# The first three passes of a software-pipelined attention and expert kernel in another order: loads of the first tile's keys and values ahead of the next tile's stores, split weights made in the third pass

## The chip, the cores and the metric

The kernel runs on one core of one Trainium2 chip. The metric is the device time of one execution in microseconds (us); lower is better. A core has five engines, each with its own instruction queue: TensorE (PE, with its weight loads shown apart as PEld), VectorE (DVE), ScalarE (ACT), GpSimd (POOL) and SyncE (SP), which here issues nearly all DMAs. Engines meet only at semaphores.

## The reference, cut to what matters

`x` is 4 x 2048 x 256 in fp32. Two blocks follow each other, each with a residual:

```python
x = x + attn(_layernorm(x))     # below
x = x + ffn(_layernorm(x))      # 8 experts, the best 2 by a gate on the mean over the sequence

def attn(q_x):                  # 16 heads of 16
    xn = ln(q_x, ln1_w, ln1_b)
    q, k, v = (xn @ w + b for w, b in ((wq, bq), (wk, bk), (wv, bv)))
    fq, fk = elu(q) + 1, elu(k) + 1
    kv = einsum('bhnd,bhne->bnde', fk, v)        # over the heads of one position
    qkv = einsum('bhnd,bnde->bhne', fq, kv)
    qk = einsum('bhnd,bnd->bhn', fq, fk.sum(axis=1))
    a = (qkv / (qk[..., None] + 1e-6)) merged to (b, n, 256)
    x = q_x + a @ wo + bo
    h = gelu(ln(x, ln2_w, ln2_b) @ fc_w + fc_b)  # 256 -> 1024
    return x + h @ proj_w + proj_b
```

## The kernel before, in words

The 8192 positions are cut into 16 tiles of 512. The work on a tile is cut into named stages, and a pass (`iterations`, L59) is a list of stage names; `LAG` (L44) says how many passes behind the pass number the tile of a stage is, so one pass holds early stages of one tile, middle stages of the tile before, and so on. The order is written out by hand. `walk` (L153) goes through all passes and stages, and every engine's program is made by one such walk: an engine takes from each stage the part that is its own, in this one order. A wait is on a count that the walk keeps (`at(name)`): the number of increments of that semaphore by all stages that stand earlier in the order, whatever tile they belong to. So the place of a stage also decides what its waits cover.

The stages that matter here, by tile (t is the tile's number):

- `L:t` SP loads the input tile. `DS:t`, `D1:t`: DVE statistics and normalisation into `xhat` (L598), POOL the power -1/2 (L423).
- `X:t`: PE transposes `xhat` into the PSUM banks `sa` (L828), ACT copies them to `xhT` (L470).
- `DV:t`: PE makes the values in `sa` (L872), ACT copies them to `feat_v` (L480) after a wait on `v_out` (L477), that is on all value stores so far, since there is one `feat_v`; POOL adds the bias (L430); SP stores them to `scratch_v` in 8 DMAs (L327).
- `DQ:t`, `DK:t`: PE makes queries (banks `pw`) and keys (banks `sa`) (L881), ACT the two halves of elu (L488, L489), DVE joins them in `fqk` (L651), SP stores them to `scratch_q`, `scratch_k`, 2 DMAs each (L333).
- `K0:t`, `K1:t`: SP loads one half of the queries and keys back in another layout, 8 DMAs (L356), after waits on all stores `q_out` and `k_out` that stand earlier in the order (L351-352). `VL:t`: SP loads the values back into `vb`, 8 DMAs (L345), after `v_out` (L337).
- `B0`, `B8`: PE makes the scores of the first half (L892) in the four banks of `ps`, which are `sa` and `sb`; DVE masks them into `am` (L658). `B1`: the weighted sum of the first half into `sa` (L905), ACT to `ot` (L513). `B2`: scores and mask of the second half. `B3`: its weighted sum.
- `NS0`, `NS1`: SP stores a half of `ot` to `scratch_nd` (L363). `NL0`, `NL1`: SP loads it back as numerators and denominators `nd`, 3 DMAs (L369). `N0`: DVE divides the first half; `N`: the second half, then the split of `attnT` (L687, L690, L697, L698).
- `Y`, `YB`: the residual (DVE, POOL). `A2:t`: PE multiplies with `wo` (L986), DVE adds and takes statistics. `R`, `H`, `SA`: second norm, its transposes (L828), the sum on POOL.
- `M1` to `M4` (from the fourth pass on): the MLP of one tile (L936 up, L920 down) together with B1 to B4 of the next. `F1` to `F2`: experts.
- `WV`: once, the bias of the values. `WS`: once, the MLP bias with `ln2_b` folded in (PE, 32 small matmuls, L850, after which DVE adds them at L631), `ln2_w` folded into `fc_w` (L633), and `wo`, `fc_w` and `proj_w` split into two fp32r parts each (L641, L643). `A2` of tile 0 waits for the splits (`split_done`).

The first passes hold fewer stages than the later ones, since the pipeline fills. The lag of `K0`, `K1`, `VL`, `B0`, `B8` is 1 and that of `Y`, `A2`, `N` and the like 2, so pass 2 is the one in which tile 0 reaches `A2` and pass 3 is the first with the MLP. In pass 2, `B1` to `B3` and `NS0` to `NL1` are those of tile 0, `VL`, `K0`, `K1` those of tile 1, and `X`, `DV`, `DQ`, `DK` those of tile 2.

Of the kernel before, what the change touches and what calls it, by code (L numbers as in the profile page):

```python
# [8 lines left out]
H, HD = 16, 16  # L9
# [7 lines left out]
SUB = T // P  # L17
# [23 lines left out]

LAG = {"L": 0, "DS": 0, "D1": 0, "X": 0, "DV": 0, "DQ": 0, "DK": 0, "K0": 1, "K1": 1, "VL": 1, "B0": 1, "B8": 1,  # L44
       "Y": 2, "YB": 2, "NS0": 2, "NL0": 2, "NS1": 2, "NL1": 2, "N0": 2, "N": 2, "A2": 2, "R": 2, "SA": 2, "H": 2, "J7": 3, "JA": 3, "XS": 4, "J2": 4, "Z": 4, "E": 4,
       "XL": 7, "F1": 7, "F3": 7, "F4": 7, "FX": 7, "F2": 7}
TAIL = ["DV", "DQ", "DK", "A2", "F1", "R", "B0", "F3", "F4", "SA", "H", "B8", "FX", "F2"]
HEAD_TAIL = ["XL", "E", "X", "J7", "JA", "YB", "G", "N", *TAIL]
FULL_TAIL = ["XL", "X", "J7", "JA", "YB", "E", "N", *TAIL]
MERGED = ["L", "XS", "M1", "J2", "Y", "NS0", "M2", "NL0", "K0", "DS", "Z", "M3", "NS1", "D1", "M4", "NL1", "VL", "N0", "K1"]  # L50
EARLY = ["L", "M1", "Y", "NS0", "M2", "NL0", "K0", "DS", "M3", "NS1", "D1", "M4", "NL1", "VL", "N0", "K1", "X", "J7", "JA", "YB",
         "N", "DV", "DQ", "A2", "R", "DK", "SA", "B0", "B8", "H"]


def experts(t):
    return [f"F1:{t}", f"F3:{t}", f"F4:{t}", f"FX:{t}"]


def iterations():  # L59

    yield 0, ["WV", "DS:0", "L:1", "D1", "X", "DV", "DS:1", "DQ", "L:2", "D1:1", "DK"]
    yield 1, ["X", "K0", "WS", "VL", "DV", "DQ", "DS:2", "DK", "D1:2", "B0", "B8", "K1"]
    yield 2, ["K0", "Y", "B1", "NS0", "X", "DV", "B2", "NL0", "DQ", "B3", "NS1", "NL1", "VL", "N0", "K1",
              "DK", "YB", "N", "A2", "R", "SA", "B0", "B8", "H"]
    yield 3, EARLY
    for i in range(4, 7):
        yield i, [
            s for t in EARLY for s in {"L": ["L", "XS"], "Y": ["J2", "Y"], "M3": ["Z", "M3"], "YB": ["YB", "E"]}.get(t, [t])]
    for i in range(7, TILES):
        yield i, MERGED + (HEAD_TAIL if i % PER_BATCH == PER_BATCH - 1 else FULL_TAIL)  # L70
    yield 16, ["XS", "M1", "J2", "Y", "NS0", "M2", "NL0", "K0", "Z", "M3", "NS1", "M4", "NL1", "VL", "N0", "K1", "XL",
               "J7", "JA", "YB", "E", "N", "F1", "F3", "F4", "A2", "R", "SA", "B0", "B8", "H", "FX", "F2"]
    yield 17, ["XS", "M1", "J2", "Y", "NS0", "M2", "NL0", "Z", "M3", "NS1", "M4", "NL1", "N0", "XL",
               "J7", "JA", "YB", "E", "N", "F1", "F3", "F4", "A2", "R", "SA", "H", "FX", "F2"]
    yield 18, ["XS", "C1", "J2", "C2", "Z", "C3", "C4", "XL:11", "J7", "JA", "E", "XS:15", "J2:15", "F1:11", "Z:15", "F3:11",
               "F4:11", "FX:11", "E:15", "F2:11", "G:15", "XL:12"]
    yield 19, experts(12)
    for t in range(13, TILES):
        yield t + 7, [f"F1:{t}", f"F2:{t - 1}", f"XL:{t}", *experts(t)[1:]]
    yield 23, ["F2:15"]  # L80
# [7 lines left out]
def rounds(name):  # L88
# [26 lines left out]
    "varz_ready": {"J2": 1}, "rstdz_ready": {"J2": 1},  # L115
    "xhat_ready": {"D1": 1},
    "f_ready": {"DQ": NC, "DK": NC},
    "q_out": {"DQ": 32}, "k_out": {"DK": 32}, "v_out": {"DV": 16 * 2 * SUB},
    "kq_in0": {"K0": 32 * NQ}, "kq_in1": {"K1": 32 * NQ}, "v_in": {"VL": 32 * TA},
    "nd_out": {"NS0": 16, "NS1": 16}, "num_in0": {"NL0": 48}, "num_in1": {"NL1": 48},  # L120
    "attnT_ready": {"N": 1},
# [18 lines left out]
class Place:  # L140


    def __init__(self, name, i, base, names):
        self.stage, _, t = name.partition(":")
        self.i, self.base = i, base
        self.t = int(t) if t else i - LAG[self.stage] if self.stage in LAG else None
        self.sum_pending = self.stage in ("F1", "F2") and names[0].startswith("F1") and names[1].startswith("F2")

    def at(self, name, more=0):
        return self.base[name] + more  # L150


def walk(run):  # L153

    base = {name: by.get("P", 0) for name, by in INC.items()}
    for i, names in iterations():
        for name in names:
            place = Place(name, i, base, names)
            run(place)
            base = {sem: value + INC[sem].get(place.stage, 0) for sem, value in base.items()}  # L160


def build(nc, x, wqkv, wo, fcw, pjw, gw, ew, eb, cols, rows, ident_d, mask_d, out):
# [7 lines left out]
    with ctx:  # L171
# [106 lines left out]
        def waiter(eng):  # L278

            def wait(name, value):  # L280
                if value > 0:
                    eng.wait_ge(S[name], value)
            return wait
# [11 lines left out]
        def _(sp):  # L295
            wait = waiter(sp)
# [8 lines left out]
            def run(p):  # L305
                at = p.at
# [10 lines left out]
                if p.stage == "XL":  # L317
                    wait("x2_out", at("x2_out"))
                    wait("out_stored", at("out_stored"))
                    sp.dma_start(out_sb[:, :, :], x2_dram[p.t]).then_inc(S["x2_in"], 16)  # L320
                if p.stage == "DV":
                    wait("v_in", at("v_in", -INC["v_in"]["VL"]))
                    dst = v_dram[p.t % VRING].rearrange("(s b k g) d -> s b g k d", s=SUB, b=2, k=KG)
                    for s in range(SUB):
                        wait("v_ready", at("v_ready", s // 2 + 1))
                        for b in range(2):
                            sp.dma_start(dst[s, b], feat_v[P // 2 * b:P // 2 * (b + 1), s]).then_inc(S["v_out"], 16)  # L327
                if p.stage in ("DQ", "DK"):
# [55 lines left out]
                if p.stage == "F2":  # L384
                    for u in range(2):
                        wait(f"pj_free{u}", at(f"pj_free{u}", 1))
                    sp.dma_start(out_t[p.t], out_sb[:, :, :]).then_inc(S["out_stored"], 16)

            walk(run)
            sp.wait_ge(S["out_stored"], 16 * (TILES + 1))  # L390

# [419 lines left out]
        def _(pe):  # L811
            wait = waiter(pe)
# [4 lines left out]
            def run(p):  # L817
                at = p.at

                def empty(name, *more):  # L820

                    for c in range(2):
                        wait(f"{name}_free{c}", at(f"{name}_free{c}", *more))

                def transposed(bank, src, c):

                    for s in range(SUB):
                        last = nc.tensor.transpose(bank[:, P * s:P * (s + 1)], src[:, s, P * c:P * (c + 1)], ident[:, :])  # L828
                    return last

                def transposes(name, banks, src):

                    for c in range(NC):
                        wait(f"{name}_free{c}", at(f"{name}_free{c}"))
                        transposed(banks[c], src, c).then_inc(S[f"{name}_full{c}"], 1)
# [21 lines left out]
                    last.then_inc(S["pw_full0"], 1)  # L857
                if p.stage == "X":
                    wait("xhat_ready", at("xhat_ready"))
                    transposes("sa", sa, xhat)  # L860
                    features_copied[:] = [at(f"sa_free{c}", 1) for c in range(NC)]
                if p.stage in ("DV", "DQ", "DK"):
# [84 lines left out]
                elif p.stage[0] in "BCM" and p.stage not in ("B0", "B8"):  # L947
# [16 lines left out]
                    if "B" in parts and r == 0:  # L964
                        empty("sa")
                        if p.i == LAG["NS0"]:
                            pe.wait_ge(const_done, 4 + 2 * NQ)
# [55 lines left out]
                if p.stage == "F2":  # L1023
                    wait("acc_ready", at("acc_ready", -NC if p.sum_pending else 0))
                    for u in range(2):
# [6 lines left out]
                        last.then_inc(S[f"pj_full{u}"], 1)  # L1032

            walk(run)


# [42 lines left out]
```

## Time and profile before

| | |
|---|---|
| median of 3 runs | 1098.13 us (1096.04 to 1101.01) |
| the profiled execution | 1095.77 us, of which the span of its trace is 1093.9 us |
| PE busy | 953.9 us, 87% of the span |
| DVE busy | 701.5 us, 64% |
| ACT busy | 472.2 us, 43% |
| POOL busy | 238.4 us, 22% |
| DMA | 120.85 MB, mean 110 GB/s |
| chain that ended last | PE 65%, DVE 18%, issue 8%, DMA 3%, ACT 3% |

The page also cuts the span into 40 slices of 27.3 us. PE's busy tenths in the first eight are 4, 7, 6, 4, 8, 8, 8, 9, and from there on mostly 8 and 9. All moments below are in us from the start of the span. A wait is put down in the trace to the engine or DMA that came last. The granted TensorE clock is given as a share of its full 2.4 GHz: 1.00 is that level, 0.50 is 1.2 GHz.

### The profile page before, as it was taken

Reading aid. Unit: us, or ns where it says so; the run is one execution under the profiler, and the core shown is the slowest. Engines: PE = TensorE matmul, PEld = TensorE weight load, DVE = VectorE, ACT = ScalarE, POOL = GpSimd, SP = SyncE. Lnnn points to the kernel's source line nnn. Section 1 sums busy time; section 2 is a strip of 40 time slices with the busy share of each in tenths; the row PEclk is TensorE's granted clock in tenths of the full one; section 3 lists DMA queues with packets and bytes.
Section 4 is the critical chain, followed back from the end, with each engine's and each line's share of the span. In section 5 each row is a group of like instructions: output and inputs, shape, how many; then the busy total and the mean of one; then the engine's idle time right before and its main releaser. Section 6 shows DMA issues by size and latency. Waiting matters only on the chain.

```text
span 1093.9 us, 29184 instructions
## 1 busy us (share of the span) xinstructions
PE 953.9 (87%) x12212; PEld 737.0 (67%) x12212; DVE 701.5 (64%) x1560; ACT 472.2 (43%) x738; POOL 238.4 (22%) x144
## 2 busy tenths in 40 slices
PE   4764888989698989999999989999999899897866
PEld 3543776768586767768686857777777768685633
DVE  2724565766557567777868586777777775856523
ACT  2321444535253444545545434545454454342422
POOL 3220132311314131312222131223131220312000
PEclk9866887989698889999999999999999899898979
DMA  5667354555545465565656574565666555431013
GB/s 178 106 131 120 85 91 100 98 117 95 119 89 91 105 121 122 104 159 88 150 108 130 125 131 113 112 148 107 143 107 137 110 112 116 93 88 58 33 64 116
DMA packets 428696, 120.85 MB, mean 110 GB/s; under 512 B 389904, under 2 KB 414608, under 8 KB 428304
## 3 DMA queue, kind: packets, MB, share of 16 engines
q1 hardware_dynamic: 426256, 116.83, 50.9%
q10 hardware_dynamic: 2304, 2.11, 0.7%
q8 instruction: 98, 1.61, 0.6%
q14 instruction: 38, 0.31, 0.1%
HBM read 60.17 MB, written 58.72 MB: 109 GB/s over the span
## 4 chain that ended last, share of the span: by engine, by line
PE 65%; DVE 18%; issue 8%; DMA 3%; ACT 3%; POOL 2%; SPq 1%; ACTq 0%; DVEq 0%; POOLq 0%
PE pw L936 18%; PE pj L920 13%; PE ps L892 7%; PE pw L840 5%; PE ps L986 4%; PE pj L840 4%; PE ps L905 4%; DVE nd L690 4%; DVE nd L687 4%; PE ps L872 3%; PE ps L881 2%; DVE hT L698 2%; DVE x_sb L723 2%; DVE hT L697 2%; PE pj L1030 1%
## 5 line engine op out<-in xcount | busy, mean ns | idle before, releaser
L936 PE MATMUL pw<-hT,w_fc 128*128 128x512 f32 x768 | 213.7, 419 | 10.4 <-DVE hT L678 10.4
L920 PE MATMUL pj<-w_pj,hidden 128*128 128x256 f32 x1536 | 208.7, 285 | 2.7 <-DVE hidden L671 2.7
L920 PEld LDWEIGHTS pj<-w_pj,hidden 128*128 128x128 f32 x1536 | 197.5, 190 | 14.1 <-DVE hidden L671 3.7
L671 DVE TENSOR_TENSOR hidden<-xhT,hidden 128x512 fp32r<-128x512 f32 x128 | 88.5, 692 | 165.2 <-ACT hidden L506 165.1
L505 ACT ACTIVATE xhT<-pw,col 128x512 f32<-128x512 f32 x128 | 87.8, 686 | 228.4 <-PE pw L936 227.0
L936 PEld LDWEIGHTS pw<-hT,w_fc 128*128 128x128 f32 x768 | 144.3, 199 | 43.0 <-DVE hT L678 12.1
L658 DVE TENSOR_TENSOR am<-ps,mask 128x512 f32<-128x512 f32 x128 | 79.3, 681 | 63.7 <-PE ps L892 63.7
L892 PE MATMUL ps<-kq 16*64 16x64 f32 x4096 | 87.8, 314 | 20.9 <-issue 10.9
L892 PEld LDWEIGHTS ps<-kq 16*64 16x64 f32 x4096 | 77.3, 210 | 42.4 <-issue 40.4
L986 PE MATMUL ps<-w_o,hT 128*128 128x256 f32 x384 | 61.5, 326 | 31.6 <-DVE hT L698 31.1
L506 ACT ACTIVATE hidden<-pw,col 128x512 fp32r<-128x512 f32 x128 | 87.1, 680 | 0.0
L986 PEld LDWEIGHTS ps<-w_o,hT 128*128 128x128 f32 x384 | 57.3, 229 | 43.7 <-DVE hT L698 28.5
L436 POOL TENSOR_TENSOR x<-x,row 128x1024 f32<-128x1024 f32 x16 | 37.7, 2354 | 216.3 <-DVE x_sb L723 216.3
L513 ACT ACTIVATE ot<-ps,den_eps 128x512 f32<-128x512 f32 x64 | 69.4, 1192 | 33.7 <-PE ps L905 32.7
L872 PE MATMUL ps<-w_qkv,xhT 128*128 128x256 f32 x256 | 70.2, 436 | 3.2 <-ACT xhT L470 3.2
L840 PE MATMUL pw<-zT,w_e 128*128 128x512 f32 x128 | 60.6, 618 | 8.1 <-DMA b_e<-in_eb 8.1
L430 POOL TENSOR_TENSOR feat_v<-feat_v,bv 128x512 f32<-128x512 f32 x32 | 52.7, 1664 | 56.1 <-ACT feat_v L480 56.1
L872 PEld LDWEIGHTS ps<-w_qkv,xhT 128*128 128x128 f32 x256 | 56.0, 225 | 13.0 <-issue 2.6
L840 PE MATMUL pj<-zT,w_e 128*128 128x512 f32 x128 | 58.7, 601 | 5.5 <-DVE out_sb L804 5.5
L651 DVE SCALAR_TENSOR_TENSOR fqk<-elu 128x512 f32<-128x512 f32 x64 | 44.4, 716 | 28.1 <-ACT elu L489 28.1
L687 DVE RECIPROCAL nd<-nd 128x256 f32<-128x256 f32 x32 | 55.8, 1744 | 8.9 <-DMA nd<-scratch_nd 8.9
L423 POOL TENSOR_TENSOR rs<-var,mhalf 128x8 f32<-128x8 f32 x16 | 28.2, 1764 | 151.8 <-DVE var L613 151.8
(108 smaller groups left out, 1307.8 us busy)
## 6 DMA issues: line engine op xcount, KB each, us to landing
scratch_nd<-ot SPq DMA_DIRECT2D x32, 512.0 KB, 4.4
nd<-scratch_nd SPq DMA_DIRECT2D x96, 128.0 KB, 2.6
x_sb<-in_x SPq DMA_DIRECT2D x16, 512.0 KB, 5.8
scratch_v<-feat_v SPq DMA_DIRECT2D x128, 64.0 KB
scratch_q<-fqk SPq DMA_DIRECT2D x32, 256.0 KB, 4.7
scratch_k<-fqk SPq DMA_DIRECT2D x32, 256.0 KB, 5.5
kq<-scratch_q SPq DMA_DIRECT2D x128, 64.0 KB, 3.1
kq<-scratch_k SPq DMA_DIRECT2D x128, 64.0 KB, 3.0
```

Source lines behind the costliest of these rows:

```text
L505: nc.scalar.activation(gelub[:, u], pw[u], ACT.Gelu, bias=b_fc[:, m:m + 1])
L506: nc.scalar.activation(hidden[:, m % SLOTS, 0], pw[u], ACT.Gelu, bias=b_fc[:, m:m + 1]).then_inc(S[f"pw_free{u}"], 1)
L513: nc.scalar.activation(dst[:, r // 2, v], src, ACT.Identity, bias=den_eps[:, :]).then_inc(S[f"sa_free{v}"], 1)
L658: last = nc.vector.tensor_tensor(am[:, j].rearrange("p (k n) -> p k n", n=BLOCK), ps[:, j].rearrange("p (k n) -> p k n", n=BLOCK), mask[:, ...
L671: nc.vector.tensor_tensor(hidden[:, m % SLOTS, 1], gelub[:, u], hidden[:, m % SLOTS, 0].bitcast(f32), ALU.subtract).then_inc(S["rest_ready ...
L687: link(nc.vector.reciprocal(d, d))
L840: last = nc.tensor.matmul(bank, w[:, c, P * m:P * (m + 1)], zT[:, p.t % RING, c], start=(c == 0), stop=(c == NC - 1))
L872: last = nc.tensor.matmul(sa[u][:, D * s:D * (s + 1)], xhT[:, c, P * (2 * u + s):P * (2 * u + s + 1)], w_qkv[:, 2, c], start=(c == 0), sto ...
L892: last = nc.tensor.matmul(ps[BLOCK * v:BLOCK * (v + 1), j, BLOCK * k:BLOCK * (k + 1)], kd[rows, b, cols], qd[rows, b, cols], start=True, s ...
L920: last = nc.tensor.matmul(pj[u][:, D * s:D * (s + 1)], hidden[:, m % SLOTS, a, lo:lo + P], w_pj[:, b, m], start=(m == 0 and n == 0 and s = ...
L936: last = nc.tensor.matmul(pw[bank], w_fc[:, b, c, P * m:P * (m + 1)], hT[:, a, c], start=(n == 0), stop=(n == len(order) - 1))
L986: last = nc.tensor.matmul(sb2[u][:, D * s:D * (s + 1)], attnT[:, a, c, lo:lo + P], w_o[:, b, c], start=(c == 0 and n == 0), stop=(c == NC ...
```

## The change

The stores of the values get a stage of their own, `VS`, which only SP takes part in; in all passes but the first three it stands right behind `DV`, where the stores were. Passes 1 and 2 are put in another order. PE's part of `X` gets a wait on `sc_free`, that is on the last masking of scores.

```diff
-LAG = {"L": 0, "DS": 0, "D1": 0, "X": 0, "DV": 0, "DQ": 0, ...
+LAG = {"L": 0, "DS": 0, "D1": 0, "X": 0, "DV": 0, "VS": 0, "DQ": 0, ...
-TAIL = ["DV", "DQ", "DK", ...
+TAIL = ["DV", "VS", "DQ", "DK", ...
 EARLY = [...
-         "N", "DV", "DQ", "A2", "R", "DK", "SA", "B0", "B8", "H"]
+         "N", "DV", "VS", "DQ", "A2", "R", "DK", "SA", "B0", "B8", "H"]
@@ def iterations():
-    yield 0, ["WV", "DS:0", "L:1", "D1", "X", "DV", "DS:1", "DQ", "L:2", "D1:1", "DK"]
-    yield 1, ["X", "K0", "WS", "VL", "DV", "DQ", "DS:2", "DK", "D1:2", "B0", "B8", "K1"]
-    yield 2, ["K0", "Y", "B1", "NS0", "X", "DV", "B2", "NL0", "DQ", "B3", "NS1", "NL1", "VL", "N0", "K1",
-              "DK", "YB", "N", "A2", "R", "SA", "B0", "B8", "H"]
+    yield 0, ["WV", "DS:0", "L:1", "D1", "X", "DV", "VS", "DS:1", "DQ", "L:2", "D1:1", "DK"]
+    yield 1, ["X", "K0", "VL", "K1", "DV", "DQ", "DS:2", "VS", "DK", "D1:2", "B0", "B8"]
+    yield 2, ["X", "DV", "Y", "B1", "NS0", "DQ", "B2", "NL0", "WS", "B3", "NS1", "N0", "DK", "K0", "NL1",
+              "VS", "YB", "N", "VL", "A2", "R", "K1", "SA", "B0", "B8", "H"]
@@ INC
-    "q_out": {"DQ": 32}, "k_out": {"DK": 32}, "v_out": {"DV": 16 * 2 * SUB},
+    "q_out": {"DQ": 32}, "k_out": {"DK": 32}, "v_out": {"VS": 16 * 2 * SUB},
@@ SP
-                if p.stage == "DV":
+                if p.stage == "VS":
                     wait("v_in", at("v_in", -INC["v_in"]["VL"]))
                     dst = v_dram[p.t % VRING].rearrange("(s b k g) d -> s b g k d", s=SUB, b=2, k=KG)
                     for s in range(SUB):
-                        wait("v_ready", at("v_ready", s // 2 + 1))
+                        wait("v_ready", at("v_ready", s // 2 - 1))
@@ PE
                 if p.stage == "X":
                     wait("xhat_ready", at("xhat_ready"))
+                    wait("sc_free", at("sc_free"))
                     transposes("sa", sa, xhat)
```

## Rows read from the trace of the kernel before

**Rows 1.** Stretches of 10 us: length, busy us and instructions by engine, clock, DMA.
```profile
core 0: us, PE busy (x) PEld busy (x) DVE busy (x) ACT busy (x) POOL busy (x), PEclk, DMA share, GB/s
...
90.00:100.00 10.00, 0.00 (x0) 0.00 (x0) 4.71 (x7) 0.00 (x0) 0.00 (x0) 0.50 0.61 104
...
140.00:150.00 10.00, 10.00 (x67) 9.23 (x66) 7.22 (x13) 5.91 (x9) 0.16 (x1) 1.00 0.60 109
```

**Rows 2.** Timeline of the SP queue, 20 to 115 us: start, length, what.
```profile
43.78 8.06 SPq L345 DMA_DIRECT2D vb<-scratch_v  x8
51.89 5.46 SPq L327 DMA_DIRECT2D scratch_v<-feat_v  x8
57.39 2.17 SPq L333 DMA_DIRECT2D scratch_q<-fqk  x2
59.60 3.60 SPq L333 DMA_DIRECT2D scratch_k<-fqk  x2
66.69 1.72 SPq L356 DMA_DIRECT2D kq<-scratch_q  x4
68.45 1.82 SPq L356 DMA_DIRECT2D kq<-scratch_k  x4
...
75.13 6.71 SPq L327 DMA_DIRECT2D scratch_v<-feat_v  x8
...
92.41 1.47 SPq L369 DMA_DIRECT2D nd<-scratch_nd  x3
```

**Rows 3.** Timeline of all engines, 50 to 122 us: start, length, engine, line, what, [idle].
```profile
56.84 2.07 PE L905 MATMUL ps<-am,vb 64*32 64x64 f32 x128 [3.88 <-DMA vb<-scratch_v]
...
66.51 0.60 ACT L480 ACTIVATE feat_v<-ps 128x512 f32<-128x512 f32 x1 [3.56 <-PE ps L872]
...
73.15 2.44 PE L892 MATMUL ps<-kq 16*64 16x64 f32 x128 [5.03 <-DMA kq<-scratch_k]
...
75.52 5.70 PE L881 MATMUL pw<-xhT,w_qkv 128*128 128x512 f32 x8
...
96.03 1.75 DVE L687 RECIPROCAL nd<-nd 128x256 f32<-128x256 f32 x1 [5.19 <-DMA nd<-scratch_nd]
97.82 0.76 DVE L690 TENSOR_TENSOR nd<-nd 128x256 f32<-128x256 f32 x2
...
100.71 5.46 PE L986 MATMUL ps<-w_o,hT 128*128 128x256 f32 x24 [12.97 <-DVE hT L698]
...
115.30 5.41 PE L936 MATMUL pw<-hT,w_fc 128*128 128x512 f32 x12 [1.71 <-DVE hT L678]
...
120.65 1.48 PE L905 MATMUL ps<-am,vb 64*32 64x64 f32 x128
```

**Rows 4.** The same timeline, the work of WS and what lies beside it.
```profile
31.82 3.73 PE L850 MATMUL pw<-col,zT 128*128 128x1 f32 x32
...
38.25 1.22 DVE L641 CAST w_fc<-zT 128x2048 fp32r<-128x2048 f32 x1
...
39.50 2.29 DVE L643 TENSOR_TENSOR w_fc<-zT,w_fc 128x2048 fp32r<-128x2048 f32 x1
39.82 5.31 POOL L430 TENSOR_TENSOR feat_v<-feat_v,bv 128x512 f32<-128x512 f32 x2 [13.13 <-ACT feat_v L480]
...
41.71 2.29 DVE L641 CAST w_pj<-zT 128x2048 fp32r<-128x2048 f32 x1
...
44.04 3.24 DVE L643 TENSOR_TENSOR w_pj<-zT,w_pj 128x2048 fp32r<-128x2048 f32 x1
```

**Rows 5.** A later pass, SP queue: eight value stores.
```profile
464.90 5.42 SPq L327 DMA_DIRECT2D scratch_v<-feat_v  x8
```

**Rows 6.** The same pass, ACT: the copy that waited for these stores.
```profile
472.17 1.26 ACT L545 ACTIVATE feat_v<-pw,b_e 128x512 f32<-128x512 f32 x2 [1.17 <-DMA scratch_v<-feat_v]
```

**Rows 7.** The first 3.5 us of the queries' products of tile 2: PEclk 0.50.
```profile
75.50:79.00 3.50, 3.50 (x8) 1.51 (x5) 2.48 (x4) 0.00 (x0) 0.00 (x0) 0.50 0.86 165
```

**Rows 8.** A stretch of 2 us in which only query and key stores were moving.
```profile
60.00:62.00 2.00, 1.90 (x8) 1.44 (x8) 0.00 (x0) 1.57 (x2) 0.00 (x0) 0.50 0.96 145
```

More of the change, by code:

```diff
@@ L37 @@
 DEN_EPS = 1e-6
-LAG = {"L": 0, "DS": 0, "D1": 0, "X": 0, "DV": 0, "DQ": 0, "DK": 0, "K0": 1, "K1": 1, "VL": 1, "B0": 1, "B8": 1,
+LAG = {"L": 0, "DS": 0, "D1": 0, "X": 0, "DV": 0, "VS": 0, "DQ": 0, "DK": 0, "K0": 1, "K1": 1, "VL": 1, "B0": 1, "B8": 1,
        "Y": 2, "YB": 2, "NS0": 2, "NL0": 2, "NS1": 2, "NL1": 2, "N0": 2, "N": 2, "A2": 2, "R": 2, "SA": 2, "H": 2, "J7": 3, "JA": 3, "XS": 4, "J2": 4, "Z": 4, "E": 4,
        "XL": 7, "F1": 7, "F3": 7, "F4": 7, "FX": 7, "F2": 7}
-TAIL = ["DV", "DQ", "DK", "A2", "F1", "R", "B0", "F3", "F4", "SA", "H", "B8", "FX", "F2"]
+TAIL = ["DV", "VS", "DQ", "DK", "A2", "F1", "R", "B0", "F3", "F4", "SA", "H", "B8", "FX", "F2"]
 HEAD_TAIL = ["XL", "E", "X", "J7", "JA", "YB", "G", "N", *TAIL]
```

## The prediction

> **What bounds the kernel now.** I read the page's slices first: from about 110 us on PE is busy for 8 to 9 tenths of nearly every slice, so the body is PE's, and the change leaves its order alone. Next the stretches of 10 us: between 140 and 150 PE works all the time, between 90 and 100 it does nothing at all [rows 1]. The edit lies wholly in that thin head, so I ask one question: when does the first `wo` product (stage A2 of tile 0) start, and does anything behind it come to wait for something new? Before, it starts at 100.71, last released by DVE's split of `attnT` [rows 3]. From there on the chain is A2, statistics, H, the first up product at 115.30, then the body.
>
> How it got to 100.71, read backwards through the timeline and the SP queue: DVE began the second division at 96.03, when the loads of `nd` landed [rows 3]; those were issued at 92.41 [rows 2], after the store of the second half of `ot` had landed; that store needed B3; B3 needed the scores of the second half, which ran at 73.15 because their `kq` loads landed then [rows 3]. Those loads (K1) stand behind the second tile's key stores in the queue: issue began at 66.69, though the first tile's data had long been in DRAM [rows 2]. A second late arrival is `vb` at 56.84 [rows 3]. DVE's 11.7 us for WS, from 35.6, the end of PE's part, to 47.28 [rows 4], lie before that moment and cost little: PE waits for `vb` longer.
>
> **The change part by part**, in moments of the new span.
>
> K1 moves ahead. K0 and VL keep their places, VL at 43.78 to 51.84. K1 is 8 DMAs, 3.6 us as from 66.69 to 70.27 [rows 2], so the queue is free at 55.5. Its data land by about 60, well before anyone needs them. By itself this takes the wait at 73.15 away, more than 10 us.
>
> What is queued behind it: q stores 2.2 us (to 57.7), then the 8 value stores of tile 1. These took 5.46 us in one place and 6.71 behind a large store [rows 2]; with 512 KB of q stores in front I take the middle, 6.1, so to 63.8 (63.2 to 64.4). Their landing: a later pass has the last of eight stores issued at 470.32 [rows 5] and the copy that waits for them starting at 472.17 [rows 6], 1.85 us. So `v_out` is full at 65.7. Before, these stores were issued by 57.35 and nobody waited.
>
> WS leaves pass 1. PE's 3.7 us and DVE's 11.7 us go [rows 4]. Tile 1's values, queries and keys come some 2.5 to 4 us earlier, the first scores start at about 46.6 (K0's loads, issued just ahead of VL, take about 3 us to land: between the end of K1's issues at 70.27 and the scores at 73.15 lie as many [rows 2, 3]), the mask ends by 52. The new wait on `sc_free` keeps PE's transposes of tile 2 until then, since scores fill the `sa` banks too. That is behind the old order's mask in any case; I cost it at nothing, as the next wait covers it: PE is through tile 2's values by 59 at the slower clock.
>
> The new wait. In pass 2, X and DV of tile 2 now stand ahead of B1. ACT's copy into `feat_v` needs `v_out`, tile 1's stores among them, so it starts at 65.7; before, it started at 66.51 with the stores long landed [rows 3]. But now B1 is behind it: B1 needs `sa` empty. Two copies of 0.6 us: B1 at 66.9, where it was at 56.84. Here 10 us are lost.
>
> From B1 on. B1 2.0 us, PE free at 68.9, `ot` and the first store by 71.5. Queries of tile 2: 5.6 us, as the 5.70 at 75.52 [rows 3] (the granted clock was 0.50, that is 1.2 GHz, in their first 3.5 us [rows 7], after 5 us in which PE had idled; here it idles for some 8), to 74.5. Scores of the second half 2.4, to 76.9, masked by 79.4. WS on PE 3.7, to 80.6. B3 follows; its result is stored by 85.
>
> WS on DVE. From 35.6 to 41.79 it ran at its own pace, 6.2 us; the cast of `w_pj` took 2.29 where the equal one of `w_fc` took 1.22, and its subtraction 3.24 where 2.29 stood, both while POOL added the value bias [rows 4]. At 80.7 POOL has its work behind it (from 66.5 on two bias additions, 5.3 us at the worst, and two residual sums), so I take 1.2 and 2.3: 9.6 us in all, to 90.3. The upper end is the 11.7 measured. The Trainium skill, "GPSIMD Engine Reference", Specifications, calls GpSimd's SBUF interfaces shared with VectorE, with contention for instructions in a 2-port mode or with two SBUF inputs. By that rule the sum would be 9.6 where POOL is idle and up to 11.7 where it is not; the rows agree in that direction.
>
> N0 is next on DVE: 1.75 and 0.76 [rows 3], to 92.8. Then the joins of tile 2's keys, 0.7 each, 93.5 and 94.2. **Behind these stands the SP queue**: its order is now NS1, DK, K0, NL1. The key stores wait for the joins, and K0, though it fetches tile 1, waits for all key stores before it. Four stores of q and k took from 57.39 to the start of K1 at 66.69 [rows 2], 9.3 us; at 145 GB/s [rows 8] one MB is 7.3 of them, so two stores are 3.7 plus the 2.0 that are left: from 93.5 to 99.2. For the same two stores the Trainium skill, "DMA: Bandwidth & Descriptors", Anatomy of one DMA, would give 2.0 us plus bytes by 436 GB/s, 3.2 us, and A2 2.5 us earlier; the fixed part agrees with my 2.0, the rate does not with the row's 145, so the row stands. K0's 8 issues 3.6, to 102.8; NL1 1.5, to 104.3; landing 2.15 as from 93.88 to 96.03 [rows 2, 3], 106.5. N, from there to A2, took 4.7 (96.03 to 100.71): **A2 at 111.2, 10.5 us later**.
>
> Behind A2. B1 of tile 1 comes 19.9 us after A2 [rows 3], at 131.2. The queue owes it value stores (6 us, 110.5), their landing 1.9, VL 8.1 (120.5) and 4.8 to land (from 51.84 to the end of B1's wait [rows 2, 3]): 125.4, so 5.8 us of slack. K1 follows with more. Everything else in pass 3 is issued by the same order as before. So the 10.5 us reach the end.
>
> The sum: 1095.8 + 10.5 = 1106.3 against the profiled execution; that one stands 2.4 us under the median of the runs shown, so 1108.6 against 1098.1. A measurement can tell about 0.5% here, 5.5 us.
>
> Bounds of the terms: value stores -0.6 to +0.6; queries at the full clock -2; WS +2.1; key stores' landing -0.7 to +1.6; NL1 behind eight loads +1. Together about +7 to +15.5.
>
> **Rivals.** (1) *The store wait does not bind.* If `feat_v` were free when PE is through with tile 2's values, B1 would start at 59.5, 7.4 us earlier, and PE would hardly idle, so the queries could take 3.6: A2 at about 102, +1 to +3 us, no difference that can be told. For it: in pass 2 of before the stores gave no wait. Against it: the last value store is the eighth behind 51.84 + 3.6 + 2.2, so hardly before 62.3. It decides if the v stores land before 59. (2) *Faster: the head start is kept.* The K1 loads come early, the wait at 73.15 goes and B3's store with it moves forward. Were the queue to reach NL1 before DVE asks for it (by about 85, and with B1 at 59.5), only DVE's own work would stand before A2: queries to 65, scores 67.4, WS 71.1, then 9.6 + 2.5 + 1.3 + 4.7, so about 90: 10 us faster, 1088. Against it: NL1 is behind the key stores, and those behind WS on DVE. (3) *A larger loss in pass 3*: v stores and VL at their slow ends, and their loads after all late for B1 at 131; beyond the 5.8 us of slack each us counts, 1112 to 1116. For it: the queue's work from NL1 on is nearly gapless for 20 us. Against: the slack is more than the spread of the rows. That the change does not do what it says is no case: the orders are lists, and each engine follows them.
>
> **How the numbers follow.** My forecast 0.76, rival 1 0.12, rival 2 0.06, rival 3 0.06. Slower by over 0.5%: 0.82; within: 0.12; faster: 0.06. The range: from 1101 (the good end of the terms, and the worse end of rival 1) to 1114 (the bad end, and the beginning of rival 3); rival 2 and the tails are left out.
>
> **What would show it.** Right: ACT's L480 of tile 2 waiting for `scratch_v` until 65 to 66.5; the first L905 at about 67; L643 of `w_pj` ending near 90; SP's key stores at 93.5, K0 at 99, NL1 at 103; L986 at 109 to 113; then 14.6 us to L936 and the body as before. Wrong: L905 before 62, or L986 before 103, would mean that a store wait is shorter than I read it. If L986 is at 111 and the time is not up by 10 us, something behind A2 had slack that I did not see; if the body differs, the forecast is wrong in kind.

## The result and the profile after

The changed kernel took 1113.37 us (median of 4 runs, 1109.48 to 1116.65) against 1097.09 us (4 runs, 1095.77 to 1101.01): the ratio is 1.0148, interval 1.0112 to 1.0185, so about 16 us slower. The profiled execution took 1114.79 us, its span is 1112.9 us. A second measurement of the same kernel gave 1.0161 (1.0096 to 1.0226).

The waits of the first 135 us of the changed kernel (who waited for what: us in total, times, longest):

```profile
PE ps L987 <- DVE hT L698: 21.7, 1, 21.7
...
ACT feat_v L480 <- DMA scratch_v<-feat_v: 12.5, 1, 12.5
DVE nd L687 <- DMA nd<-scratch_nd: 12.2, 1, 12.2
...
PE ps L906 <- issue: 2.4, 1, 2.4
```

Two of these lines have no counterpart of their size before: ACT's copy waits 12.5 us for value stores, and DVE waits 12.2 us for the second `nd` load (5.19 in [rows 3]). Both end in the first line, PE's 21.7 us ahead of the `wo` product. The SP queue, which [rows 2] show before:

```profile
51.84 2.46 SPq L356 DMA_DIRECT2D kq<-scratch_q  x4
54.34 1.82 SPq L356 DMA_DIRECT2D kq<-scratch_k  x4
56.20 2.02 SPq L333 DMA_DIRECT2D scratch_q<-fqk  x2
58.27 6.14 SPq L327 DMA_DIRECT2D scratch_v<-feat_v  x8
...
88.81 0.55 SPq L363 DMA_DIRECT2D scratch_nd<-ot  x1
97.69 1.36 SPq L333 DMA_DIRECT2D scratch_k<-fqk  x2
102.87 1.72 SPq L356 DMA_DIRECT2D kq<-scratch_q  x4
104.63 1.82 SPq L356 DMA_DIRECT2D kq<-scratch_k  x4
106.50 1.52 SPq L369 DMA_DIRECT2D nd<-scratch_nd  x3
```

The store of the second half is issued at 88.81 and could have landed by 93; the load of what it stored is issued at 106.50. Between them the queue waits at the key stores until 97.69, for DVE, and at K0 until 102.87, for those stores. And the timeline, against [rows 3]:

```profile
66.33 1.08 ACT L480 ACTIVATE feat_v<-ps 128x512 f32<-128x512 f32 x2 [12.47 <-DMA scratch_v<-feat_v]
...
67.52 1.79 PE L906 MATMUL ps<-am,vb 64*32 64x64 f32 x108 [8.18 <-ACT feat_v L480]
...
71.70 0.64 PE L906 MATMUL ps<-am,vb 64*32 64x64 f32 x20 [2.39 <-issue]
...
72.27 6.50 PE L882 MATMUL pw<-xhT,w_qkv 128*128 128x512 f32 x8
...
78.70 2.40 PE L893 MATMUL ps<-kq 16*64 16x64 f32 x128
...
81.03 3.73 PE L850 MATMUL pw<-col,zT 128*128 128x1 f32 x32
...
92.18 2.29 DVE L643 TENSOR_TENSOR w_pj<-zT,w_pj 128x2048 fp32r<-128x2048 f32 x1
...
110.48 1.75 DVE L687 RECIPROCAL nd<-nd 128x256 f32<-128x256 f32 x1 [12.22 <-DMA nd<-scratch_nd]
...
115.17 4.74 PE L987 MATMUL ps<-w_o,hT 128*128 128x256 f32 x24 [21.73 <-DVE hT L698]
...
129.04 4.63 PE L937 MATMUL pw<-hT,w_fc 128*128 128x512 f32 x12 [1.71 <-DVE hT L678]
...
133.60 1.48 PE L906 MATMUL ps<-am,vb 64*32 64x64 f32 x128
```

The `wo` product of tile 0 begins at 115.17, 14.5 us later than before, the first up product 13.7, the `wo` product of tile 1 12.9 (171.81 against 158.89). The B1 of tile 1 at 133.60 waits for nothing: the values of tile 1 were there. The last `wo` product is 19.1 us later (1008.10 against 988.94), so this execution also lost 6.2 us in a body whose order is the same. The experiments take the head first, then the body.

### The profile page after: what moved, and what is told of

Its sections match the earlier page's. It is cut to its first block, busy times and chain, and to the rows that moved or that the text cites. A ratio compares the mean times of both kernels' runs of the same rounds, so it can differ in the third digit from the quotient of the medians.

```text
span 1112.9 us, 29184 instructions
## 1 busy us (share of the span) xinstructions
PE 958.5 (86%) x12212; PEld 739.0 (66%) x12212; DVE 701.6 (63%) x1560; ACT 473.3 (43%) x738; POOL 235.4 (21%) x144
## 4 chain that ended last, share of the span: by engine, by line
PE 64%; DVE 17%; issue 9%; DMA 2%; ACT 2%; SPq 2%; POOL 2%; ACTq 0%; DVEq 0%; POOLq 0%
PE pw L937 18%; PE pj L921 13%; PE ps L893 7%; PE pw L840 5%; PE ps L987 4%; PE pj L840 4%; DVE nd L690 4%; PE ps L906 4%; DVE nd L687 4%; PE ps L882 2%; PE ps L873 2%; DVE hT L698 2%; DVE x_sb L723 2%; DVE hT L697 1%; PE pj L1031 1%
## 5 line engine op out<-in xcount | busy, mean ns | idle before, releaser
L873 PEld LDWEIGHTS ps<-w_qkv,xhT 128*128 128x128 f32 x256 | 56.3, 226 | 14.5 <-issue 2.6
L687 DVE RECIPROCAL nd<-nd 128x256 f32<-128x256 f32 x32 | 55.8, 1745 | 12.2 <-DMA nd<-scratch_nd 12.2
L840 PE MATMUL pj<-zT,w_e 128*128 128x512 f32 x128 | 58.7, 601 | 5.5 <-DVE out_sb L804 5.5
L430 POOL TENSOR_TENSOR feat_v<-feat_v,bv 128x512 f32<-128x512 f32 x32 | 50.0, 1579 | 57.6 <-ACT feat_v L480 57.6
```

The costliest lines, as they stand in the source:

```text
L687: link(nc.vector.reciprocal(d, d))
L840: last = nc.tensor.matmul(bank, w[:, c, P * m:P * (m + 1)], zT[:, p.t % RING, c], start=(c == 0), stop=(c == NC - 1))
L873: last = nc.tensor.matmul(sa[u][:, D * s:D * (s + 1)], xhT[:, c, P * (2 * u + s):P * (2 * u + s + 1)], w_qkv[:, 2, c], start=(c == 0), sto ...
```

## The experiments

Theory Q: the head's loss is two waits of queue order in series, the value stores ahead of B1 and the key stores and K0 ahead of NL1. In each experiment I read the moment of the first two `wo` products (tile 0, tile 1) in the trace. The edits are to the lists of passes 1 and 2. First the two medicines, one by one and together, beside the changed kernel itself.

**The changed kernel once more.** 

> The changed kernel once more, for its head and its body on this chip. The first wo product began at 115.2 where it began at 100.7 before (14.5 later), the third tile's 12.4 later, and the last tile's 19.1 later. Theory Q (two queues): the head's loss, 12 to 15 us at the first wo product, returns in every execution. Rival C (clock): the 7 us that came between the seventh and the ninth tile are the granted clock's falls in that one execution, so here the body's part lies elsewhere or is smaller; the time is 11 to 19 us over before. If the body's part comes at the same place with the same size, C falls.

Measured: 115.13 and 171.44, so the head returns to a few tenths of a us. 1111.89 us, ratio 1.0161 (1.0096 to 1.0226). From the second to the last `wo` product 832.6 us, where the first execution took 836.3 and the kernel before 830.1. The head repeats, the body does not.

**Value stores first** (pass 1 of the changed kernel).

```diff
-    yield 1, ["X", "K0", "VL", "K1", "DV", "DQ", "DS:2", "VS", "DK", "D1:2", "B0", "B8"]
+    yield 1, ["X", "K0", "VL", "DV", "VS", "K1", "DQ", "DS:2", "DK", "D1:2", "B0", "B8"]
```

> Pass 1 of the changed kernel with the value stores of tile 1 (VS) ahead of K1 and of the query stores; all else as changed. Theory Q: the stores are issued from about 51.8 to 57.3 and land by 59.3, so the copy into feat_v starts at 59 to 60 and not at 66.3, the first weighted product at 60 to 61, and all behind it in the head moves by 6 to 8 us: first wo product at 107 to 109, time 6 to 8 us under the changed kernel, still 7 to 9 over before. Rival C, that PE's gaps and low clock in the weighted product and the queries make the loss and not the store wait: the first wo product moves by 3 us or less.

Two lines of its timeline:

```profile
51.91 5.00 SPq L327 DMA_DIRECT2D scratch_v<-feat_v  x8
...
59.96 1.30 PE L906 MATMUL ps<-am,vb 64*32 64x64 f32 x108 [1.69 <-ACT feat_v L480]
```

B1 at 59.96 and the first `wo` product at 107.48: 7.7 us earlier. What remains is the same picture, 12.2 us of DVE waiting for `nd`. The store wait is shown as a cause, with its size, and rival C falls. It is shorter here but not gone: ACT's copy still waits 5.6 us. The time, 1109.69 us and ratio 1.0113 (1.0047 to 1.0179), is too loose to see 7 us.

**NL1 first** (pass 2 of the changed kernel).

```diff
-    ... "B3", "NS1", "N0", "DK", "K0", "NL1", "VS", "YB", ...
+    ... "B3", "NS1", "NL1", "N0", "DK", "K0", "VS", "YB", ...
```

> Pass 2 of the changed kernel with the second nd load (NL1) ahead of the key stores (DK) and the query and key loads (K0) in the SP queue; all else as changed. Theory Q: NL1 is issued at about 93 to 94 (store of 88.8 landed), its data are there when DVE comes to N, so the second division follows the key joins at 98.3 without the 12.2 us of waiting, and the first wo product begins at 103, 12 us earlier. From there 3 us may be given back, since the value loads of tile 1 land at about 126 and the third pass asks for them at 123: time 9 to 12 us under the changed kernel. Rival W, the DVE time of WS is the loss whatever the queue does: 3 us or less.

The first `wo` product came at 102.70, 12.5 us earlier: the second wait is shown too, and DVE's time for WS alone is not the loss (rival W falls). The give-back came as well, PE waited 3.2 us for `vb` in pass 3, and tile 1's `wo` product was 5.7 us earlier only (166.12). Behind that wait PE ran for 7 us at a mean granted clock of 0.55. 1108.30 us, ratio 1.0118 (1.0057 to 1.0180): 3.6 us under the changed kernel once more, where I had expected 9 to 12.

**Both.** 

> Both edits at once. Theory Q: the two waits are in series, so they add: first weighted product at 60 to 61, the queue out of the way, first wo product at 90 to 96, which is 5 to 10 us before the place it had in the kernel before. But the value loads of tile 1 then land at 115 to 119 and the third pass asks for them at 110 to 116, a new wait of up to 5 us: time 2 to 9 us under before. Rival O, the two overlap (either alone gives what both give): first wo product at 103 or later, time 2 us or more over before.

Of its waits between 40 and 135 us:

```profile
PE ps L987 <- DVE hT L698: 9.2, 1, 9.2
...
PE ps L906 <- DMA vb<-scratch_v: 4.4, 1, 4.4
```

First `wo` product at 94.74, 20.4 us earlier than in the changed kernel, and 7.7 + 12.5 = 20.2: the two waits are in series and add. That is 6.0 us ahead of the kernel before, yet the second line is the bill: the values of tile 1 stand behind the key stores, K0 and the value stores, and B1 of pass 3 waits 4.4 us for them. Tile 1's `wo` product is 1.4 us ahead of before (157.54), and the time the same: 1098.19 us, ratio 1.0020 (0.9982 to 1.0057). The 2 to 9 us under before that I had expected did not come.

**WS back in pass 1** (the changed kernel otherwise).

```diff
-    yield 1, ["X", "K0", "VL", ...
+    yield 1, ["X", "K0", "WS", "VL", ...
-    yield 2, [... "NL0", "WS", "B3", ...
+    yield 2, [... "NL0", "B3", ...
```

> The changed kernel with WS where it was before (pass 1, behind K0); all else as changed. Theory Q: WS on DVE in pass 2 holds N0 and with it the key joins, which the queue waits for; without it the joins of tile 2 end at about 92 to 93 and not at 98.3, since then PE's key products are the last, so the key stores, K0 and NL1 come 4 to 6 us earlier: first wo product at 109 to 111, time 4 to 6 us under the changed kernel, still 8 to 10 over before. Rival W, WS is the whole loss: first wo product at 105 or earlier. Rival 0, the slower pass 1 (DVE busy until 47) is handed on and eats it: 113 or later.

First `wo` product at 107.04, 8.1 us earlier, more than I expected and less than rival W. The key stores went out at 88.63 and not at 97.69, 9.1 us earlier, for two reasons. DVE came to the key joins without the 9.6 us of WS ahead of them. And PE was earlier with the keys, by 5.2 us (82.72 against 87.97), since it had no products of WS to do there and B1 ran without the gap of 2.4 us. So the place of WS is a part of the loss, handed on by the queue. 1101.90 us, ratio 1.0039 (1.0015 to 1.0063): 4 us over before, where I had expected 8 to 10.

**K1 alone moved, in the kernel before.** This is the part of the change that looks like pure gain.

```diff
-    yield 1, ["X", "K0", "WS", "VL", "DV", "DQ", "DS:2", "DK", "D1:2", "B0", "B8", "K1"]
+    yield 1, ["X", "K0", "WS", "VL", "K1", "DV", "DQ", "DS:2", "DK", "D1:2", "B0", "B8"]
```

> The kernel before with K1 alone moved, to just behind VL in pass 1, so the stores of tile 1 come after it. My reading: the scores of the second half no longer wait until 73.15 for their loads and follow the values of tile 2 at 68.3, so the third weighted product and all behind it move by 4 to 5 us: first wo product at 96 to 97, time 4 to 5 us under before. Rival: the nd loads behind the value stores of tile 2 then end the wait, and the gain is 1 us or less.

Its timeline, PE's B3 and the SP queue behind it:

```profile
77.27 1.64 PE L905 MATMUL ps<-am,vb 64*32 64x64 f32 x128
...
77.36 5.66 SPq L327 DMA_DIRECT2D scratch_v<-feat_v  x8
83.06 1.55 SPq L369 DMA_DIRECT2D nd<-scratch_nd  x3
84.66 2.17 SPq L333 DMA_DIRECT2D scratch_q<-fqk  x2
86.94 2.02 SPq L363 DMA_DIRECT2D scratch_nd<-ot  x1
92.49 1.46 SPq L369 DMA_DIRECT2D nd<-scratch_nd  x3
```

My expectation failed and its rival held. PE's B3 came 3.9 us earlier (77.27 against 81.15), but its store stood behind 8 value stores, the first `nd` load and the query stores, and went out at 86.94 where it went at 87.09 before. First `wo` product at 100.68, to 0.03 us where it was. The queue, not the data, was the bound. The time, 1094.40 us with a ratio of 0.9967 (0.9940 to 0.9995), is a gain that the head does not show; the next two runs say how such a figure is to be read.

**A delay in the head of the kernel before.** In pass 2, DVE does two reciprocals into free buffers ahead of the second division. They are extra work; nothing of the computation is left out.

```diff
                 if p.stage == "N":
+                    if p.i == 2:
+                        wait("num_in1", at("num_in1"))
+                        wait("yb_ready", at("yb_ready"))
+                        nc.vector.reciprocal(hn[:, :, :], x1[:, :, :])
+                        nc.vector.reciprocal(out_sb[:, 0:3], x1[:, 0:3])
                     divided(1)
```

> The kernel before, order untouched, with 12.2 us of extra DVE work (two reciprocals into free buffers) between the landing of the second nd load and the second division of pass 2. Nothing else waits for it. It moves the first wo product from 100.7 to about 113, as the change did. Theory H (head only): the time rises by 12 to 13 us and the body is as long as before. Rival S (shift): a later start of the body makes the body itself longer, as it seems to be in the changed kernel by 2 to 6 us: the time rises by 15 us or more. If H holds here, the changed kernel's other 3 to 5 us belong to something else in it.

The two took 11.3 us, the first `wo` product moved by 11.0 us (111.67), tile 1's by 9.1. The median of 9 runs is 11.5 us above that of before; the ratio of 1.0090 (1.0050 to 1.0131) makes it 10 us, 5.5 to 14. H, 12 to 13 us for a delay of 12.2, fits. S as I wrote it, 15 us or more, falls; but the delay was 11 us, and a body longer by 2 to 5 us still lies inside the interval. Yet the profiled execution, the slowest of the nine (1114.22 us), lost another 9.6 us in the body.

**PE's new wait alone, in the kernel before.**

```diff
                     wait("xhat_ready", at("xhat_ready"))
+                    wait("sc_free", at("sc_free"))
                     transposes("sa", sa, xhat)
```

> The kernel before with nothing but PE's wait on sc_free ahead of the transposes of X in all passes. I costed it at nothing: within 2 us of before. Rival: the wait costs in the body (one more PE instruction in 16 passes, or transposes held back), 3 us or more over before, spread over the tiles; this would then be the part of the loss that the head does not explain.

1096.72 us, ratio 0.9993 (0.9969 to 1.0018), and every `wo` product within 2 us of its old place. In this kernel the wait costs nothing that could be told (-3 to +2 us), as I had taken it, so the body's loss is hardly its doing.

**The body.** Stretches of 5 us in the changed kernel's execution, after tile 7, with the busy us of PE first and the granted clock as the third figure from the end:

```profile
core 0: us, PE busy (x) PEld busy (x) DVE busy (x) ACT busy (x) POOL busy (x), PEclk, DMA share, GB/s
...
560.00:565.00 5.00, 4.41 (x102) 3.86 (x103) 0.53 (x1) 0.00 (x0) 0.00 (x0) 0.76 0.41 96
565.00:570.00 5.00, 5.00 (x20) 4.47 (x19) 3.34 (x9) 1.27 (x2) 0.00 (x0) 0.55 0.64 157
570.00:575.00 5.00, 5.00 (x150) 4.38 (x149) 3.22 (x15) 2.33 (x4) 1.73 (x1) 1.00 0.10 28
```

and the place that answers to it in the kernel before, some 12 us earlier:

```profile
545.00:550.00 5.00, 5.00 (x145) 4.24 (x143) 2.26 (x8) 1.26 (x2) 1.26 (x1) 1.00 0.95 282
550.00:555.00 5.00, 5.00 (x32) 4.45 (x32) 4.51 (x11) 1.81 (x3) 0.00 (x0) 1.00 0.48 115
555.00:560.00 5.00, 5.00 (x153) 4.51 (x153) 2.56 (x13) 3.51 (x6) 1.73 (x1) 1.00 0.28 75
```

The work is the same. But in the changed kernel's execution PE stood still in the middle of one group of scores:

```profile
560.60 0.75 PE L893 MATMUL ps<-kq 16*64 16x64 f32 x24 [1.67 <-issue]
```

The profile shows nothing that it waited for, and after it the granted clock fell to 1.2 GHz for some 7 us. In the kernel before the same group ran through without a pause and the clock stayed at 1.00; so it did in the changed kernel's second execution. Seven of the 12 traces have this standstill: the clock fell behind the three of 1.67 to 2.00 us and not behind the four of 0.51 to 1.28 us.

I added up, over stretches of 2 us, the time at 1.2 GHz between the second and the last `wo` product, for the 12 executions of which I have the trace. It goes from 74 us (K1 alone) over 88 (before), 94 and 97 (the changed kernel, twice) to 104 (the delay) and 111 (value stores first), and the body's length goes with it: 827.1, 830.1, 832.6, 836.3, 839.7 and 839.4 us. The other six lie between, and one is off this line: WS back, with 94 us at 1.2 GHz like the changed kernel's second execution, has 837.5 us, 4.9 us more. So a body is up to 12 us longer or shorter in an order that is the same, mostly with the clock; standstills like the one above are in it too. Whether a later head makes the clock fall more often stays open: the six executions whose second `wo` product was over 4 us late had bodies of 832.6 to 839.7 us, the six others 827.1 to 836.1, and with one execution each that is no proof. The test by time is the delay run, which says no more than some 5 us either way. The clocks of all its executions do not decide it either: from their means, 175 us at 1.2 GHz (9 executions) against 165 in the kernel before (32 executions beside it), and of these 10 us 4 lie ahead of the second `wo` product in the traces.

**A version with all of it.** Both edits; WS first in pass 2, where DVE and PE idled; K0 and VL ahead of the stores of tile 2.

```diff
-    yield 2, ["X", "DV", "Y", "B1", "NS0", "DQ", "B2", "NL0", "WS", "B3", "NS1", "N0", "DK", "K0", "NL1",
-              "VS", "YB", "N", "VL", "A2", "R", "K1", "SA", "B0", "B8", "H"]
+    yield 2, ["WS", "X", "DV", "Y", "B1", "NS0", "DQ", "B2", "NL0", "B3", "NS1", "K0", "NL1", "VL", "N0", "DK",
+              "VS", "YB", "N", "A2", "R", "K1", "SA", "B0", "B8", "H"]
```

> The changed kernel with both edits of before (value stores of tile 1 ahead of K1; NL1 ahead of the key stores), and in pass 2 also WS first of all stages, K0 between NS1 and NL1, VL behind NL1 and the key and value stores of tile 2 after it. Theory Q: DVE's 9.6 us for WS fall into its idle time between 52 and 69, so the third weighted product comes at 72 to 74, the second nd load at 81 and lands by 85, the first wo product begins at 88 to 91, 10 to 12 us before its place in the kernel before; the value loads of tile 1 land by 97, so the third pass waits for nothing: time 7 to 13 us under before. Rival: the value loads ahead of other work delay NL1's data or the key loads, first wo product at 95 or later and no gain.

The SP queue in its pass 2:

```profile
80.53 0.56 SPq L363 DMA_DIRECT2D scratch_nd<-ot  x1
81.21 3.25 SPq L356 DMA_DIRECT2D kq<-scratch_q  x4
84.50 2.16 SPq L356 DMA_DIRECT2D kq<-scratch_k  x4
86.70 1.52 SPq L369 DMA_DIRECT2D nd<-scratch_nd  x3
```

1090.51 us, ratio 0.9941 (0.9913 to 0.9970): faster than before by some 6 us, and over 20 us faster than the changed kernel. The head is as my rival had it, not as I had: first `wo` product at 95.31, since NL1 went out at 86.7 and not at 81. Most of that is B3, which began at 76.40 where I had expected 72 to 74, so that its store went out only at 80.53: even in the next run, where nothing stands between the store and NL1, NL1 went out at 84.79. The rest is K0, whose issues took 5.4 us and not 3.6. Tile 1's is 6.1 us ahead of before (152.75), and nobody waits for `vb`. PE's small WS products took 7.9 us there and not 3.7, which held X back by 4 us: PE stood still for 1.5 us after the fifth of the 32 (shown as issue), and the other 27 ran at a granted clock of 0.50, where they had run at 0.95 in the kernel before. In time against the kernel before, this is the gain that the head shows.

**The same with NL1 ahead of K0.** 

> As e7_all, with NL1 ahead of K0 instead of behind it. In e7_all the second nd load was issued at 86.7 behind 5.5 us of query and key loads, and the first wo product began at 95.3. Here it is issued when the store of 80.5 has landed, at about 85, so its data land by 87.5 and the first wo product begins at 91 to 93; K0 and VL end 4 us later, landing at about 103 against a need at 111. Time 2 to 5 us under e7_all, 8 to 13 under before. Rival: the value loads then come too late and give it back, no difference to e7_all.

From its timeline, the SP queue and DVE:

```profile
84.79 1.71 SPq L369 DMA_DIRECT2D nd<-scratch_nd  x3
86.64 1.81 SPq L356 DMA_DIRECT2D kq<-scratch_q  x4
...
90.83 1.75 DVE L687 RECIPROCAL nd<-nd 128x256 f32<-128x256 f32 x1 [2.48 <-DMA nd<-scratch_nd]
```

A miss: NL1 was issued 1.9 us earlier, but its data were there at 90.8 as well, 4.3 us after the end of its issues. With the value loads behind it this had been 2.2 us (kernel before) and 2.4 (all of it), with the value stores 2.5 (changed kernel). The query and key loads right behind it are what is different here, and they explain only a part. Over all `nd` loads of the 12 traces, from the end of issue to the landing, the spread is wide: with query and key loads issued right behind them the median is 2.9 us (157 cases, 2.3 to 5.2), with value loads 2.1 us (173 cases, 2.0 to 4.9). So 4.3 is at the long end of either kind; what made it so long here is open. First `wo` product at 95.52; 1090.59 us, ratio 0.9938 (0.9903 to 0.9972), the same as its neighbour.

All together, in us against the kernel before (the interval is that of the ratio, times 1097):

| kernel | `wo` of tile 0 | `wo` of tile 1 | time |
|---|---|---|---|
| changed | +14.5 | +12.9 | +12 to +20 |
| changed, again | +14.4 | +12.6 | +11 to +25 |
| value stores first | +6.8 | +4.9 | +5 to +20 |
| NL1 first | +2.0 | +7.2 | +6 to +20 |
| both | -6.0 | -1.4 | -2 to +6 |
| WS back in pass 1 | +6.3 | +6.0 | +2 to +7 |
| delay in before | +11.0 | +9.1 | +6 to +14 |
| wait on `sc_free` in before | -0.1 | -0.3 | -3 to +2 |
| K1 alone in before | 0.0 | -0.1 | -7 to -1 |
| all of it | -5.4 | -6.1 | -10 to -3 |
| all, NL1 ahead of K0 | -5.2 | -6.8 | -11 to -3 |

The time goes with the second column; where that lies outside the interval, for K1 alone and for the value stores first, it is by half a us or less. One thing is not even, though. The four kernels that were measured beside the same 13 executions of before (changed again, value stores first, NL1 first, both) all have their ratio's middle above the second column, by 3.6 to 7.5 us. Those 13 had a median of 1093.44 us, the other three sets of before 1097.09 to 1098.09. How much of it is that set and how much longer bodies is not settled.

## Why the prediction was right, and where it was off

- **The sign and the two waits were right.** The stores of tile 1 were forecast at 57.7 to 63.8 and stood at 58.27 to 64.41; the copy at 65.7 began at 66.33; B1 at 66.9 began at 67.52. The key stores went out 4.2 us after the forecast, but K0 5.2 us behind them (5.7 forecast) and NL1 3.6 behind K0, as forecast. Moving the stores ahead gave 7.7 us and moving NL1 ahead 12.5 us at the first `wo` product, each by itself.
- **WS on DVE at 9.6 us** was right to a tenth: from 84.87 to 94.47. POOL was idle by then and the cast of `w_pj` took 1.22, no longer 2.29 [rows 4]. By the Trainium skill ("GPSIMD Engine Reference", Specifications) the two engines share SBUF interfaces, with contention for DVE instructions in a 2-port mode or with two SBUF inputs. The traces agree in direction: here cast and subtraction ran without POOL beside them, 1.22 and 2.29 us; in the version with all of it the cast did too, 1.22, but the subtraction had POOL's bias addition beside it and took 3.33.
- **"The key stores' landing", 5.7 us**, by the row's rate, measured 5.2. The Trainium skill's fit ("DMA: Bandwidth & Descriptors", Anatomy of one DMA), 2.0 us plus bytes by 436 GB/s, gives an estimate of 3.2 us. But the page states it for DMAs that GpSimd issues, and these came from SP, so the prediction should not have held it against the row; the measurement sides with the row.
- **The terms that were too small: "B1 2.0 us" and "Queries of tile 2: 5.6".** B1 took 4.8 from its start to the next product: after 108 of 128 matmuls PE stood still for 2.4 us with nothing to wait for that the profile shows. The queries took 6.4. Together with the copy's 0.6 us the scores began at 78.70 and not at 74.5, and this lateness, 4.2 us, is the whole distance between 111.2 and 115.2 at the `wo` product.
- **"So the 10.5 us reach the end": the head's loss did, but a term was missing.** Between the first `wo` product and the second 1.5 us came back (the `wo` and up products ran 4.74 and 4.63 us, where it was 5.46 and 5.41, at a mean granted clock of 0.61 against 0.50 and 0.51). The body then took 6.2 us more in the profiled execution and 2.5 in the second. I had no term for the body's length, and the prediction itself had said that a differing body would make it wrong in kind.
- **The range was met with luck.** The sum said +10.5 us with bounds of +7 to +15.5; measured were +16, and 1113.4 lies just inside the upper end of 1114. By its own sign, L986 at 109 to 113, the product at 115.17 came too late. The two shortfalls, 4 us in the head (of which 1.5 came back) and some 3 us behind it, pointed the same way. The time even lies in the 1112 to 1116 of rival 3, whose wait did not occur.
- **The new wait on `sc_free`, costed at nothing**: measured so in the kernel before. In the changed kernel it held PE's transposes of tile 2 until 51.01, the end of the mask, and ACT's wait of 12.5 us covered that, as the prediction had argued.
- **A statement that was wrong, though no term of the sum:** that K1 ahead of the stores takes more than 10 us away by itself. In the kernel before it takes nothing: the queue ends the wait in the data's place.
- **The rivals.** (1) The stores were not through by 59; the wait was 12.5 us. With the stores moved ahead it was still 5.6 us, and then the copy began at 59. (2) The head start was lost behind WS and the key stores, as argued; only with the queue put in order does half of it appear. (3) B1 of pass 3 waited for nothing in the changed kernel; its values landed at 126.6 and it began at 133.60. The wait it describes showed up in the experiments in which A2 came earlier than the queue could bring the values (3.2 and 4.4 us).

## What to carry to other kernels

In a pipeline whose stages are one list for all engines, moving a stage moves it in every engine's queue, and in the queue of the DMAs above all: before moving a load ahead, list what then stands behind it and which wait of an earlier tile each of these holds; here a load of tile 0 pushed stores whose landing another engine wanted, and a store of tile 2 stood ahead of the load that tile 0's product needed. A wait by count covers all that stands ahead of it in the list, whether it is needed or not, so the place of the wait decides too. And measure such a head by the moment of its last product in the trace, which returns to a few tenths of a us, where the time of the whole kernel scatters by ten.

## What the runs showed of the hardware that I had not expected

- PE stood still for 2.3 to 2.9 us at the same place, after the 108th of the 128 matmuls of B1, in all five executions of the four kernels whose PE stream was the same up to there (the changed one twice, value stores first, NL1 first, both), whenever that moment came (63.8 to 71.8 us). With WS ahead of it in the stream (kernel before, WS back, all of it) there was none at this place. But in both versions with all of it PE stood still in the middle of WS, for 1.5 and 1.4 us. Counted over all of PE's records, weight loads and sequencer included, 449 stand ahead of that standstill and 705 ahead of the one in B1, 256 more; the next one in the middle of a group, in all 12 traces, has 6082 ahead of it, 21 times 256 and one more. So it goes with the place in PE's stream; what causes it was not tried.
- The length of an unchanged body went from 827 to 840 us between executions, with 74 to 111 us of it at 1.2 GHz. The same lull is followed by more time at the lower clock in one execution than in another: PE is idle for 1.51 us ahead of the same scores in all 12 traces (229.23 in the kernel before, 242.45 in the changed kernel's second execution). Between the `wo` products on either side of it 8 of them spent 6.2 to 7.9 us at 1.2 GHz and took 58.7 to 59.2 us, the other 4 spent 16.7 to 17.3 us there and took 61.1 to 61.7.
- The same `nd` loads of three DMAs landed 2.0 to 5.2 us after the end of their issues over the 12 traces, 2.1 us in the median with value loads issued right behind them and 2.9 with query and key loads.
